# Three groups of tokens instead of two, and gated products emptied by ScalarE and multiplied by GpSimd

## The reference

```python
h = _layernorm(x) * (1 + ca) + sa                       # ca, sa, ga ... come from a small vector c
x = x + ga * attn0(h)      # 16 heads of 8, softmax over all 2048 keys
h = _layernorm(x) * (1 + cb) + sb
# ffn0: 16 experts of width 128, each token goes to its best one; and a shared expert of width 512
logits = h @ router_w.T
score = sigmoid(max(logits))                            # of the one chosen expert
gate, up = split((h * score) @ gate_up_proj[expert])    # 128 x 256 per expert
routed = (up * silu(gate)) @ down_proj[expert]
shared = (silu(h @ sgw.T) * (h @ suw.T)) @ sdw.T
x = x + gb * (shared + routed)
# layer 1
x = x + ga1 * attn1(h1)    # 8 query heads of 16, one key and value head, causal
x = x + gb1 * mix(h2)      # token mix: sigmoid(..) * (relu(..)^2 @ W_v)
```

## Time and profile before

| | us |
|---|---|
| three timed runs | 1070.91, 1078.50, 1096.03 |
| their median | 1078.5 |
| the profiled execution, its own time | 1067.41 |
| span of its trace | 1065.5 |
| mean granted clock of TensorE | 0.963 of full speed |

### The profile page before, as it was taken

One profiled execution on the slowest core, in us unless ns is written; L12 is line 12 of the kernel. 1 busy time (PEld: TensorE's weight loads), 2 busy tenths in 40 slices (PEclk: granted clock), 3 DMA queues, 4 the chain that ended last, 5 costly groups with the idle time before them and its releaser, 6 DMA issues.

```text
span 1065.5 us, 22648 instructions
## 1 busy us (share of the span) xinstructions
PE 922.1 (87%) x8934; PEld 339.6 (32%) x8934; DVE 887.4 (83%) x1133; ACT 819.6 (77%) x1587; POOL 185.4 (17%) x347
## 2 busy tenths in 40 slices
PE   5998888888888888888888899899988998788888
PEld 2552222222222222222232355333333453222224
DVE  7999999999999999999998688753688767797704
ACT  4139999998999998999986588574865566566786
POOL 4233300003000003000023200331032213201112
PEclk9779999999999999999999999996989999899999
DMA  3510400000000000000000451111100341100000
GB/s 108 160 52 3 134 17 16 2 2 2 1 2 2 2 2 2 2 1 2 2 2 24 133 151 53 40 46 36 37 2 4 118 126 29 41 10 1 1 11 12
DMA packets 41385, 37.03 MB, mean 35 GB/s; under 512 B 5084, under 2 KB 39452, under 8 KB 41280
## 3 DMA queue, kind: packets, MB, share of 16 engines
q1 hardware_dynamic: 39024, 30.20, 9.8%
q0 software_dynamic: 1824, 5.25, 1.7%
q10 hardware_dynamic: 432, 0.13, 0.0%
HBM read 21.92 MB, written 13.30 MB: 33 GB/s over the span
## 4 chain that ended last, share of the span: by engine, by line
PE 40%; DVE 35%; ACT 17%; issue 6%; POOL 1%; DMA 1%; another core or an unknown queue 0%; ACTq 0%; DVEq 0%; SPq 0%; POOLq 0%
DVE mx L1338 30%; ACT PT L1593 12%; PE O L1035 11%; PE T L1001 7%; PE T L1011 2%; PE S L1150 2%; PE S L966 2%; PE S L1116 2%; ACT PT L1587 1%; PE S L1106 1%; PE S L958 1%; PE T L916 1%; PE O L885 1%; PE S L971 1%; PE S L1107 1%
## 5 line engine op out<-in xcount | busy, mean ns | idle before, releaser
L1338 DVE TENSOR_REDUCE mx<-S 128x2 f32<-128x1024 f32 (+2 forms) x672 | 755.6, 1181 | 64.1 <-PE S L971 23.1
L1593 ACT ACTIVATE PT<-T 128x512 f32<-128x512 f32 (+2 forms) x1280 | 674.2, 580 | 111.0 <-PE T L1011 48.3
L1035 PE MATMUL O<-PT,Va 128*9 128x256 f32 (+1 forms) x4032 | 328.1, 390 | 5.4 <-ACT Os L1627 5.4
L1001 PE MATMUL T<-Qs,Ks 26*128 26x512 f16 x1024 | 201.5, 386 | 66.2 <-ACT PT L1593 49.8
L958 PE MATMUL S<-Ks,Qs 24*128 24x512 f16 x1024 | 201.0, 392 | 7.3 <-DVE mx L1338 3.0
L1001 PEld LDWEIGHTS T<-Qs,Ks 26*128 26x128 f16 x1024 | 55.5, 91 | 290.5 <-ACT PT L1593 191.6
L1035 PEld LDWEIGHTS O<-PT,Va 128*9 128x9 f32 x4032 | 67.6, 88 | 120.0 <-issue 109.2
L1035 PE MATMUL O<-PT,V 128*17 128x512 f32 (+3 forms) x616 | 76.2, 562 | 0.4 <-POOL PT L1772 0.3
L1011 PE MATMUL T<-Qs,K 50*128 50x512 f16 (+3 forms) x256 | 47.0, 360 | 25.3 <-ACT PT L1593 24.4
L966 PE MATMUL S<-K,Qs 48*128 48x512 f16 (+3 forms) x320 | 59.3, 363 | 7.4 <-DVE mx L1338 6.1
L1872 POOL TENSOR_SCALAR n<-nm 128x16 f16<-128x16 f32 x24 | 6.7, 280 | 309.4 <-DVE nm L1346 309.4
(11 more groups left out here) (325 smaller groups left out, 837.9 us busy)
## 6 DMA issues: line engine op xcount, KB each, us to landing
Wg<-in_L_ffn_experts SPq DMA_DIRECT2D x28, 192.0 KB, 2.5
Ks<-in_L_ffn_experts SPq DMA_DIRECT2D x20, 192.0 KB, 2.7
Vf<-sorted_x SPq DMA_DIRECT2D x12, 256.0 KB, 4.4
sorted_y<-Vf SPq DMA_DIRECT2D x12, 256.0 KB, 2.3
rows_q<-q SPq DMA_DIRECT2D x7, 256.0 KB, 2.3
sorted_x<-XP POOLq DMA_DIRECT2D x1, 1792.0 KB, 10.7
Qs<-nrow SPq DMA_DIRECT2D x96, 2.0 KB
Qs<-rows_q SPq DMA_DIRECT2D x8, 192.0 KB, 3.6
```

The costliest lines, as they stand in the source:

```text
L1001: m = e.matmul(bank, Ks[r0:r0 + 26, quad, keys], Qs[r0:r0 + 26, quad, CH * c:CH * c + CH], start=True, stop=True, tile_position=(r0, 0))
L1035: m = e.matmul(acc[32 * g:32 * g + d1, lo:hi], v, PT[(2 * j + g // 2) % 4][:, p0 + lo:p0 + hi], start=fresh, stop=True, skip_group_check=n ...
L1338: e.tensor_reduce(mx[:, u % 2, h0:h0 + 2, kb], two[:, :, 0:n], AX.X, ALU.max).then_inc(free, 1)
L1593: e.activation(PT[(2 * j + pair) % 4][:, CH * i + lo:CH * i + CH], bank[:, lo:CH], ACT.Exp).then_inc(free, 1)
```

## The change

1. Three groups: token tiles 0 to 7 with 24 expert tiles, 8 to 11 with 20, 12 to 15 with 20: 64 expert tiles, 32 pairs, instead of 48 and 24.
2. Placement: shared 0 and 1 begin 10 steps after their chunk's attention, with their 12 pieces 3 steps apart. Group 0 is sorted after chunk 1 and its 36 pieces go one a step, from step 153. Chunk 2 has its own group 1 (1.2 pieces a step, from step 212) and shared 2 with pieces 0.7 steps apart; group 2, for chunk 3, has 2.3 pieces a step from step 272, shared 3 is 0.6 apart. `setup1` of chunks follows its group's `gather`, which is put one step behind the group's last piece.
3. `up` and `m1` become `gate`: 256 columns of gate and 256 of up in one bank of ring T. ScalarE takes tanh of the first half and copies the whole bank into SBUF, which frees it; GpSimd makes tanh x gate, + gate, x up (three products or sums of 128 x 256). Two sets of buffers: ScalarE waits until GpSimd has done the gate two before. VectorE has no part. A shared chunk has eight gates (two halves of 256 tokens, four blocks).
4. `down` becomes four stages of 128 tokens, each in a bank of ring T, with one VectorE add each; PE waits for `gated`, GpSimd's count.

```diff
-GROUPS = ((0, 12, 0, 28), (12, 16, 28, 20))
-NT = 48
-SLOTS = (16, 8)
+GROUPS = ((0, 8, 0, 24), (8, 12, 24, 20), (12, 16, 44, 20))
+NT = 64
+GROUP_OF = (0, 0, 1, 2)
+SLOTS = (16, 16, 8)
...
+    def gated(*a):
+
+        def gate():
+            P.gate[a] = len(P.gate) + 1
+            beside("gate", *a)
+        return [gate]
+
+    def experts(s, g, per):
         n = GROUPS[g][3] // 2
...
+        pieces = []
+        for p in range(n + 2):
             if p < n:
+                pieces.append(lambda p=p: beside("m0", g, p))
+            if 0 <= p - 1 < n:
+                pieces += gated("m1", g, p - 1)
+            if 0 <= p - 2 < n:
+                pieces.append(lambda p=p: m2(p - 2))
+        def gather(s):
+            for i, c in enumerate(c for c in range(4) if GROUP_OF[c] == g):
+                at_side(s + 2 * i, lambda c=c: P.stage("gather", c))
+                setup1(s + 3 + 2 * i, c)
+
+        pieces[-1] = lambda: (m2(n - 1), gather(now[0] + 1))
+        for i, piece in enumerate(pieces):
+            at(s + int(i / per), piece)
 
     def shared(s, c, apart):
-        for bl in range(4):
-            at(s + apart * bl, lambda bl=bl: between("up", c, bl))
-        at(s + 4 * apart, lambda: between("down", c))
+        pieces = []
+        for half in range(2):
+            for bl in range(4):
+                pieces += gated("up", c, bl, half)
+            pieces += [lambda j=j: beside("down", c, j) for j in (2 * half, 2 * half + 1)]
+        for i, piece in enumerate(pieces):
+            at(s + int(i * apart), piece)
...
         elif c < 2:
             route(t + 5, c)
+            shared(t + 10, c, 3)
+            if c == 1:
+                sort(t + 11, 0)
+                experts(t + 21, 0, 1)
         elif c == 2:
-
             route(t + 2, 2)
...
+            sort(t + 8, 1)
+            shared(t + 9, 2, 0.7)
+            experts(t + 16, 1, 1.2)
         else:
             route(t + 1, 3, 2)
-            shared(t + 5, 3, 1)
-            s = sort(t + 5, 1)
-            s = experts(s, 1, 0.6)
-            at_side(s, lambda: P.stage("gather", 3))
-            setup1(s + 3, 3)
+            s = sort(t + 5, 2)
+            shared(t + 6, 3, 0.6)
+            experts(s, 2, 2.3)
...
+                elif name == "gate" and a[0] == "up":
+                    _, c, bl, half = a
                     done(("turn", 1, c))
                     pe.wait_ge(ld_w1, LD_W1)
...
+                    bank, full = opened((name,) + tuple(a))
+                    for i, w in enumerate((sgT, suT)):
+                        m = e.matmul(bank[:, 256 * i:256 * i + 256], w[:, 128 * bl:128 * bl + 128], hc(c, 256 * half, 256 * half + 256), start=True, stop=True)
+                    m.then_inc(full, 1)
                 elif name == "down":
...
+                    c, j = a
+                    bank, full = opened(("down", c, j))
                     pe.wait_ge(po_scaled, SCALED["dn"])
+                    pe.wait_ge(gated, P.gate["up", c, 3, j // 2])
                     for bl in range(4):
...
+                        m = e.matmul(bank[:, 0:128], ams[bl][:, 128 * j:128 * j + 128], sdT[:, bl, :], start=bl == 0, stop=bl == 3)
                     m.then_inc(full, 1)
...
                 elif name == "m2":
                     g, p = a
                     bank, full = opened(("m2", g, p))
-                    done(("m1", g, p))
+                    pe.wait_ge(gated, P.gate["m1", g, p])
...
+                elif name == "gate":
+                    bank, free = filled((name,) + tuple(a))
+                    if P.gate[tuple(a)] > 2:
+                        ac.wait_ge(gated, P.gate[tuple(a)] - 2)
+                    tanh, _, _, both = gate_buffers(a)
+                    e.activation(tanh, bank[:, 0:256], ACT.Tanh, scale=0.5)
+                    e.activation(both, two_tiles(bank), ACT.Copy).then_inc(free, 1)
...
+                elif name == "gate":
+                    tanh, gate, lift, _ = gate_buffers(a)
+                    done((name,) + tuple(a))
...
+                    po.tick(e.tensor_tensor(tanh, tanh, gate, ALU.mult))
+                    po.settle()
+                    po.tick(e.tensor_tensor(tanh, tanh, gate, ALU.add))
+                    po.settle()
+                    e.tensor_tensor(to, tanh, lift, ALU.mult).then_inc(gated, 1)
```

188 lines of the change are left out of this document (64 added, 124 removed).

## The result

The changed kernel is slower: 1140.5 us, the median of four runs (1136.2 to 1143.0), against 1074.7 for four of the kernel before in the same session. The ratio is 1.065, with a 95% interval from 1.054 to 1.075. I forecast 1081 and no measurable difference; the time lies outside my range too. The profiled execution took 1140.8 us, which is 73.4 more than the 1067.4 of the one before.

The account below looks back on a forecast made before the run. No engine bounds the whole: VectorE paces plain steps, TensorE's order and waits the dense stretch. Terms +6 + 28 - 36 + 5 = +3 on 1067.4 gave 1070 profiled, 1081 us on the timed scale; range 1042 to 1115.

Parts of the forecast that it names:

- The dense stretch: Steps 192 to 256, layer 0's feed-forward: bound by TensorE's order and waits, not VectorE; 249.3 us against 148.5 plain.
- Prices: Unit costs for all steps: gate 0.9 us on ScalarE, pair 1.6 us, shared chunk in the dense stretch 13.7 us.
- A: Steps 64 to 128, which gain shared 0 in 12 pieces: +6 us, between 5 and 10.
- B: Steps 128 to 192, which gain shared 1, a sort and group 0's twelve pairs: +28 us, between 22 and 38.
- 170 at 94%: Steps 128 to 192: TensorE's 170 us of work at 94% busy takes 181 us, against 153.3 before.
- C: Steps 192 to 256: 65 us over plain instead of 101, so -36 us, between -60 and -20.
- D: From step 256: VectorE's relief -5, late chunk 3 +5 and +2, GpSimd +3; together +5 us, between -10 and +20.
- Burst +5, shift +2: Maxima at five a step in steps 295 to 302 cost +5 us; unit 6's shift, late for step 304, +2.
- The six before shorter: The six steps before the maxima crowd of steps 295 to 302 would be shorter, counted within its +5 us.
- Evenly loaded: Rival, whole kernel from step 64: spread pieces let TensorE run at 94%; -28 us, 1050; chance 0.32.
- GpSimd becomes the gate: Rival, mainly shared 2 and 3: 256-column products near 1.26 us, a gate 3.5 to 4; +35 us, 1115; chance 0.14.
- Ring T too short: Rival, mostly steps 64 to 192: gates take exponentials' banks, ScalarE idles 0.4 us each; +32 us, 1112; chance 0.14.

Follow-up runs that it names:

- e2: Changed kernel with the gates multiplied by VectorE straight from the bank, only tanh on ScalarE, no copy, nothing on GpSimd: ratio 1.066 to the kernel before.
- e9: Changed kernel with two of GpSimd's three products of every gate left out: ratio 1.064 to the kernel before.
- e10: Changed kernel with two of GpSimd's three products of every gate and also ScalarE's copy left out: ratio 1.046 to the kernel before.
- e6: Kernel before with shared 0 and 1 (five wide pieces each) placed after their own chunks in steps 64 to 192: ratio 1.006 to the kernel before.
- e11: Changed kernel with m0 and m2 in one piece in group 2 alone, so chunk 3's queries come three steps earlier: ratio 1.061 to the kernel before.
- e5: Kernel before with chunk 3's new rows of layer 1 six steps later in the order, no work added: ratio 1.023 to the kernel before.
- e1: Changed kernel with the 64 gates back in ring S, ScalarE still copying and GpSimd still multiplying: ratio 1.071 to the kernel before.
- e14: Changed kernel with eight of its 32 expert pairs left out, 24 as in the kernel before: ratio 1.040 to the kernel before.
- e3: Changed kernel with the gates back in ring S and multiplied by VectorE, narrow pieces and new order kept: ratio 1.059 to the kernel before.

## Why the prediction was wrong, step by step

**The dense stretch is bound by TensorE and not by VectorE**: right as far as it was tested. With all 64 gates on VectorE (e2) steps 192 to 256 take 217.1 us, without them and with one product on GpSimd (e9) 217.5, both at a clock of 0.98. That the copy on ScalarE hides a gain from VectorE's relief is not excluded.

**Prices.** The gate on ScalarE (0.9) and the product (0.72) were right: 0.38 + 0.59 less the overlap, and 0.73. "A pair 1.6 us" was the price in the expert stretch, where TensorE is full and everything else waits beside it. In plain steps it is 2.2 to 2.4. The failed part of the step is "less the room of 0.2 a step".

**A, +6, was +12.7, and B, +28, was +48.9.** This is the step that failed by reasoning. I added ScalarE's work, subtracted its room over the steps, did the same for TensorE, and took the larger sum. TensorE's busy time in B I had at 170, and it was 169.8; ScalarE's 144.8 + 26.4 = 171, and it was 168.3. The sums of work were right. But "170 at 94%" presumes that one engine can run through. Three engines hand tiles around, and a gate makes TensorE late by 0.81 us, then ScalarE's copy the next half-step by 0.45. The delays are in series (e10 takes away the second), and room that each engine had in other half-steps is lost. A, with its shared chunk, was mis-sized in the same way: 8 x 0.9 of ScalarE less 3.2 of room for what is 13 by half-steps. ScalarE over 96% in B, my own test, came out at 83%. Shared chunks: I charged an `up` in full steps by what ScalarE gets from it, and e6 shows that five old pieces cost 10.9 there.

**C, -36, was -19.5** in one execution at a clock of 0.93. The same list took 226.1 us (-23) in e11 at 0.95, and with one product less a gate 217.5 (-32) in e9 at 0.98, with VectorE's products 217.1 in e2. So in some executions the sum came near, and a good part of the 16 us is the clock. I had expected it near 1.00: the hole without maxima tiles in steps 235 to 241 is gone in the list, the clock did not follow. The two shared chunks give back 16 to 26 (e6), for 27 as priced. ScalarE's copy is worth 7 of these steps (210.5 in e10, at e9's clock). How the rest splits between the clock and the pairs stays open.

**D, +5, was +33**, the largest miss. The mechanism stands in the prediction: pieces end later, chunk 3's queries come at 291, and the maxima are crowded at five a step from 295. "Burst +5, shift +2" measured 26 (e5: 26.3 in the same twelve steps). I had priced the burst as VectorE's steps of 5.7 us against shorter steps before, and the shift as two late steps. Left out: TensorE at the lower clock beside it, with 11.8 us without exponentials at its end, since the shift's way through memory now stands behind the last of the crowd and there is no lead left to cover it. "The six before shorter" came true for 1.5 us here and 8 in e5, whose clock was 1.00 there for 0.90. A further 8 us are steps 264 to 272 (36.3 to 44.5), where the twelve pieces of shared 3 stand closest; with one product a gate instead of three they are 38.0 (e9), so GpSimd's part, 3 in my sum, is 3.9 by TensorE's waits and 6.5 at most; the clock, 0.85 for 1.00, is the other candidate.

**The rivals.** *Evenly loaded* fell: TensorE is at 86% in A and 84% in B, not at 94%. *GpSimd becomes the gate* fell as priced: 0.73 us a product; four waits of TensorE, 8.6 us. *Ring T too short* came nearest in size (28 us over my sum in A and B, where it had 32) and it had the lateness behind a gate (0.4; measured 0.45), but as the ring's: with the gates out of ring T (e1) it stays at 2.10, and without the copy (e10) it goes.

**Where the 6.5% come from**, by ratios against the kernel before: chunk 3 late, 2.3% (e5); eight more pairs for the third group, about 2.5% (e14, which has some 0.7% of the former in it); the shared chunks in full steps, 0.6% (e6). That is some 4.7%. The rest is about 1.8%, some 19 us, and by the intervals it may be 0.4 to 3.2%. ScalarE's copy would cover it (1.8% from e9 to e10), but part of that already stands in the price of the eight pairs, and with VectorE in its place (e2, e3) the time is nearly the same. No version here beats the kernel before.

## What to carry to other kernels

Where a stage is paced by engines that hand small tiles around, room can't be added up per engine: price a new piece by the half-step it lands in, full service time of the engine that does it plus what the next engine is late by, and expect about the engine's whole busy time as the cost. Measure it by the length of single half-steps, with and without the piece; they came in five or six lengths here, where the stage's sums told little. When work moves, look first at what becomes due later because of it: a deadline missed by six of 336 steps cost 25 us here, a third of all the time that was added. A slower engine is free only at a distance: count the pieces between its product and the reader.
